# How much of the room for sorted tokens is zeroed, and when, in two routed feed-forward layers

## The chip, the core and the metric

The kernel runs on one core of a Trainium2 chip. A core has five engines with an instruction stream each: TensorE (PE, matmuls), VectorE (DVE), ScalarE (ACT), GpSimd (POOL) and SyncE (SP, which here only issues DMAs and loads registers). They meet by semaphores. DMAs run on 16 DMA engines that all issuers share. The metric is the device time of one execution in microseconds, the median of several.

## The reference

Six residual sublayers on x of 32 batches x 128 tokens x 128 channels: an attention, a cross attention, a feed-forward layer with 8 experts, then the same three once more with 16 experts. The change touches the two routed layers only. What they compute:

```python
# layer 0 (8 experts, 2 of them for each token)
t = rms_norm(x) * norm_weight                      # 4096 tokens of 128
gate_scores, expert_idx = top_k(t @ gate_w.T, 2)
weights = softmax(gate_scores)
x = x + sum over the 2 experts e: weights * (gelu(t @ W1[e].T + B1[e]) @ W2[e].T + B2[e])

# layer 1 (16 experts, 1 of them for each token)
hidden = _layernorm(x)
top_val, e = top_k(hidden @ router_w.T, 1)
g, u = split(sigmoid(top_val) * hidden @ gate_up[e])
x = x + silu(hidden @ shared_gate.T) * (hidden @ shared_up.T) @ shared_down.T + u * silu(g) @ down[e]
```

## The kernel before

One program in six stages, one for each sublayer; stage 3 is the layer with 8 experts, stage 6 the one with 16. Batches are worked on in 8 groups of 4 (G = 4). The order of the work is written out by hand in the source: each engine has its own list of pieces for each step, and a stage's opening pieces are mixed into the stage before.

**How tokens are sorted.** In DRAM lies `sorted_tokens`, a room with a region of rows for each expert (in stage 3 of 2560 rows, in stage 6 of 4096), 65536 rows of 512 bytes in all. VectorE works out for each token the row it goes to (expert times region plus the count of earlier tokens of that expert), and GpSimd scatters the tokens there, 128 with each indirect DMA (L1979 in stage 3, L3400 in stage 6). When the counts of all tokens are known, VectorE's `settle` rounds each expert's count up to whole tiles of 128 rows and makes a list of tiles: 48 of them in each of the two stages, so that a last few are spare. SyncE then loads tile numbers into a register, two at a time (L1930, L3550), and fetches the tiles into SBUF (L1932, L3552). TensorE takes them in quads of four: it flips them (L2523, L3797), multiplies them with their experts' weights, and SyncE stores the result of each quad (L1945, L3562). At the end GpSimd gathers each token's result rows (L2044, L3583), and they are added to x.

**Why zeros.** Rows of a tile behind an expert's last token hold no token. They are multiplied with the rest and nobody reads the result, but they have to hold numbers. So the whole room is zeroed from a tile of zeros (`s_zero`, L1920): its lower part ahead of stage 3 (4 transfers, ahead of GpSimd's first scatter, which waits for the semaphore `cleared`), the rest (4 transfers) behind it, and the lower part once more when stage 3 has used it (4 transfers). GpSimd's first scatter in stage 6, and the start of stage 5, wait for `regions_cleared`.

**Stage 3 in its order.** Five of the groups are sorted (their scatters lie in the last half of stage 2), three are computed densely, with every expert. TensorE does eight dense units, then the 12 quads of sorted tiles, then 16 more dense units, in which GpSimd gathers the results of the sorted groups and stage 4 is opened. A dense group begins with the flip of its tokens (L2445), then come units of hidden layer (L2505) and output (L2515), the logits (L2452), and the flip of the weights (L2460).

**Stage 6 in its order.** TensorE does 12 chunks of the shared expert, in the middle of which the last tokens are routed and `settle` runs on VectorE (its first signal is L3671); then the 12 quads, then 20 more shared chunks (L3772, L3774, L3783), during which GpSimd gathers. SyncE waits for `first_rows_ready` and for the last scatter, loads six quads ahead, and then stores a quad and loads another one in turn.

Of the kernel before, what the change touches and what calls it, by code (L numbers as in the profile page):

```python
# [1670 lines left out]
CLEARINGS = 8  # L1671
# [17 lines left out]
CLEARINGS3 = 4  # L1689
CLEARINGS_AT = {2: (0, 1), 3: (2, 3), 4: (4,), 5: (5,), 6: (6,), 7: (7,)}  # L1690
# [44 lines left out]
def stage3(nc, core, w, a, sorted_dram, done_dram, regions_cleared, before, stack):  # L1735
# [48 lines left out]
    pairs = pairs_index = place = done = None  # L1784
# [41 lines left out]
    ALL_ROWS = E6 * REGION // P  # L1826
# [88 lines left out]
    LOWER = slice(0, E3 * REGION3)  # L1915

    def clear_rows(sp, region, k, done):
        count = (region.stop - region.start) // CLEARINGS3
        piece = sorted_dram[region.start + k * count:region.start + (k + 1) * count, :]
        sp.dma_start(piece.rearrange("(p j) d -> p (j d)", p=P).rearrange("p (r c) -> p r c", c=GT),  # L1920
                     zero[:, :].unsqueeze(1).to_broadcast([P, count * D // P // GT, GT])).then_inc(done, 16)

    def by_sync(sp):
# [4 lines left out]
        def load(q):  # L1928
            for n in range(q * G, (q + 1) * G, 2):
                pair = nc.sync.value_load(pairs_index[0:1, n // 2:n // 2 + 1], min_val=0, max_val=ALL_ROWS ** 2 - 1)  # L1930
                for k, tile in enumerate((pair & (ALL_ROWS - 1), pair >> ALL_ROWS.bit_length() - 1)):
                    sp.dma_start(rows[:, (n + k) % (FLIGHTS * G), :],  # L1932
                                 tiles_dram[bass.ds(tile & (ALL_ROWS - 1), 1), :, :].rearrange("k p d -> p (k d)")
                                 ).then_inc(rows_landed[q % FLIGHTS], 16)

        sp.wait_ge(pairs_ready, 1)
        sp.wait_ge(dispatched, SORTED * G * 2 * 16)
# [282 lines left out]
    def by_vector(dve, piece, following=None):  # L2220
# [64 lines left out]
        def rank_of(g):  # L2285
# [13 lines left out]
            link(nc.vector.scalar_tensor_tensor(slot[:, :, :], index[:, batches, :], float(REGION3), rank[:, tens, :],  # L2299
# [3 lines left out]
        def settle():  # L2303
# [3 lines left out]
            def link(instruction):  # L2307
# [5 lines left out]
            dve.wait_ge(drained, turn["counts", 0] + 1)  # L2313
            link(nc.vector.tensor_scalar(padded[:, 0, :], counts[:, :], float(P - 1), None, ALU.add))
# [3 lines left out]
            link(nc.vector.tensor_scalar(gaps[:, :], padded[0:1, 1, :], -1.0, float(REGION3), ALU.mult, ALU.add))  # L2318
            tile_start = w.tile_start[:, :].unsqueeze(2).to_broadcast([1, TILES3, E3 - 1])
            link(nc.vector.tensor_tensor(passed[:, :, :],  # L2320
                                         ends[0:1, 0:E3 - 1].unsqueeze(1).to_broadcast([1, TILES3, E3 - 1]), tile_start,
                                         ALU.is_le))
            link(nc.vector.tensor_tensor(skipped[:, :, :], passed[:, :, :],
                                         gaps[:, 0:E3 - 1].unsqueeze(1).to_broadcast([1, TILES3, E3 - 1]), ALU.mult))
            link(nc.vector.tensor_reduce(owner[:, 1, :], skipped[:, :, :], AX.X, ALU.add))
            link(nc.vector.tensor_tensor(owner[:, 1, :], owner[:, 1, :], w.tile_start[:, :], ALU.add))
            link(nc.vector.tensor_scalar(owner[:, 1, :], owner[:, 1, :], float(E3 * REGION3 - P), None, ALU.min))
# [4 lines left out]
            link(nc.vector.tensor_reduce(owner[:, 0, :], passed[:, :, :], AX.X, ALU.add))  # L2332
# [296 lines left out]
    def main(following):  # L2629
        nonlocal b1_all, b2_all, h, padded, ends, starts, gaps, passed, skipped, owner, owners, owners_index, pairs, pairs_index  # L2630
        nonlocal place, done
        with ExitStack() as local:
# [8 lines left out]
            starts = late("starts", [P, E3])  # L2641
# [1320 lines left out]
```

## Time and profile before

| | |
|---|---|
| median of three runs | 1554.5 us (1547.81 to 1556.99) |
| the profiled execution's own time | 1555.21 us |
| its span, first to last instruction | 1553.4 us |
| mean granted TensorE clock | 0.965 |
| TensorE busy (matmuls) | 1429.2 us, 92% |
| VectorE, ScalarE, GpSimd busy | 59%, 53%, 43% |
| the chain that ended last | TensorE 58%, issue 14%, GpSimd 11% |
| DMA | 92.61 MB, 58.21 MB of them written to DRAM |

How to read it: the profile is of one execution, and its times are microseconds from the span's start. A row's idle time in brackets is what its engine waited just before, with what ended the wait; "issue" and "remote" say that nothing which the profile shows on this core's engines ended it. The clock column gives the granted TensorE clock as a share of 2.4 GHz (0.50 is 1.2 GHz). A row that stands for several instructions gives their count (x4). "us to landing" is the time from a DMA's issue to its completion.

### The profile page before, as it was taken

To read this page: it belongs to the slowest core of one execution; us is meant where nothing else is said; L and a number is where in the kernel's file an instruction comes from. 1 tells how busy PE (TensorE), PEld (TensorE's weight loads), DVE (VectorE), ACT (ScalarE), POOL (GpSimd) and SP (SyncE) were. 2 spreads that over 40 slices of the span, in tenths; PEclk is the share of its full clock that TensorE was granted. 3 is DMA by queue.
4 is the path that set the end of the run, shared out by engine and by line. 5 is a ranking of instruction groups with operands and counts; after the bars stand their busy time and mean duration, and the time that the engine had idled before them with its cause. 6 is when DMAs were issued, how large, how long until landed. Compare 5 with 4: busy or idle time off the path is not lost.

```text
span 1553.4 us, 38336 instructions
## 1 busy us (share of the span) xinstructions
PE 1429.2 (92%) x14613; PEld 1090.7 (70%) x14613; DVE 923.2 (59%) x2386; ACT 819.9 (53%) x1558; POOL 661.6 (43%) x679
## 2 busy tenths in 40 slices
PE   6999999996999988997968998989999999998997
PEld 5776776774777766795646666667778778775764
DVE  3343444334888864542488999965667667665223
ACT  4455455444686754453437776655554554542531
POOL 3234444434235543003478776623333444443034
PEclk9999999998999988998979999999999999999999
DMA  5020330000375631138100000000000000001323
GB/s 157 16 62 9 97 111 8 12 1 6 141 280 183 235 115 56 50 99 310 32 11 6 2 2 2 2 14 6 2 6 9 11 11 9 7 12 37 101 69 87
DMA packets 97821, 92.61 MB, mean 60 GB/s; under 512 B 21869, under 2 KB 71658, under 8 KB 97386
## 3 DMA queue, kind: packets, MB, share of 16 engines
q1 hardware_dynamic: 93034, 80.71, 16.0%
q0 software_dynamic: 4608, 9.45, 2.0%
q8 instruction: 120, 1.97, 0.5%
q14 instruction: 59, 0.48, 0.1%
HBM read 31.92 MB, written 58.21 MB: 58 GB/s over the span
## 4 chain that ended last, share of the span: by engine, by line
PE 58%; issue 14%; POOL 11%; DVE 7%; ACT 5%; DMA 3%; SPq 1%; another core or an unknown queue 1%; POOLq 0%; DVEq 0%; ACTq 0%
PE bank L3122 6%; PE bank L1538 5%; PE bank L3110 5%; PE bank L3157 4%; PE bank L1554 4%; PE bank L3136 4%; POOL s_p L1217 3%; PE bank L3148 3%; PE bank L854 2%; PE bank L2505 2%; PE bank L874 2%; PE bank L2515 2%; PE bank L827 2%; PE bank L1527 2%; POOL s_rows L3583 2%
## 5 line engine op out<-in xcount | busy, mean ns | idle before, releaser
L1324 ACT COPY s_pT<-bank 77x512 f32<-77x512 f32 (+1 forms) x256 | 136.4, 584 | 89.6 <-PE bank L1538 85.9
L2899 POOL TENSOR_TENSOR s_p<-s_p,s_inverse 128x616 f32<-128x616 f32 x64 | 78.6, 1230 | 216.0 <-DVE s_inverse L3037 216.0
L1538 PE MATMUL bank<-ident,s_p 128*77 128x128 f32 (+1 forms) x1024 | 147.5, 293 | 19.8 <-ACT s_p L1315 10.3
L1538 PEld LDWEIGHTS bank<-ident,s_p 128*77 128x77 f32 (+1 forms) x1024 | 122.0, 154 | 51.0 <-ACT s_p L1315 29.1
L1217 POOL TENSOR_TENSOR s_p<-s_p,s_peak 128x1024 f32<-128x1024 f32 x64 | 120.2, 1900 | 31.1 <-DVE s_peak L1408 31.1
L1315 ACT ACTIVATE s_p<-s_p 128x616 f32<-128x616 f32 (+1 forms) x128 | 111.0, 887 | 30.3 <-POOL s_p L1217 25.9
L720 DVE TENSOR_TENSOR s_aT<-bank,s_weight 128x512 f32<-128x512 f32 x64 | 44.3, 692 | 98.7 <-PE bank L864 82.3
L3122 PE MATMUL bank<-pos_bias,s_ctx 128*32 128x128 f32 x3072 | 91.9, 274 | 1.2 <-issue 1.2
L2957 ACT ACTIVATE s_p<-s_p 128x616 f32<-128x616 f32 x64 | 46.5, 726 | 85.7 <-DVE s_p L3025 85.7
L1394 DVE TENSOR_TENSOR s_p<-bank,pos_bias 128x1024 f32<-128x1024 f32 x64 | 77.7, 1218 | 20.9 <-PE bank L1527 20.9
L3021 DVE TENSOR_REDUCE s_peak<-bank 128x8 f32<-128x616 f32 x64 | 50.8, 794 | 62.8 <-PE bank L3136 62.8
L3122 PEld LDWEIGHTS bank<-pos_bias,s_ctx 128*32 128x32 f32 x3072 | 82.1, 110 | 6.5 <-issue 2.7
L3110 PE MATMUL bank<-s_ctx,s_kq 128*128 128x308 f32 x256 | 84.1, 437 | 1.8 <-ACT s_kT L2937 1.8
L1554 PE MATMUL bank<-s_pT,s_v 77*32 77x128 f32 (+1 forms) x2048 | 72.9, 283 | 12.9 <-DVE x_all L1441 12.0
L712 DVE TENSOR_TENSOR s_weight<-s_decay,bank 128x512 f32<-128x512 f32 x64 | 41.1, 683 | 73.4 <-ACT s_decay L560 73.4
L1527 PE MATMUL bank<-w_s_q,w_s_oT 32*128 32x308 f32 (+1 forms) x512 | 65.2, 580 | 19.0 <-POOL w_s_q L1208 15.3
L566 ACT COPY s_qT<-bank 128x512 f32<-128x512 f32 x64 | 37.5, 586 | 85.3 <-PE bank L827 85.3
L1554 PEld LDWEIGHTS bank<-s_pT,s_v 77*32 77x32 f32 (+1 forms) x2048 | 54.7, 112 | 36.8 <-issue 27.2
L3136 PE MATMUL bank<-s_kT,s_xnT 128*128 128x308 f32 x256 | 72.9, 426 | 6.3 <-ACT s_xnT L2930 6.3
L854 PEld LDWEIGHTS bank<-s_level,w_band 128*128 128x128 f32 x512 | 59.6, 191 | 26.3 <-issue 19.7
L3032 DVE TENSOR_REDUCE s_total<-s_p 128x8 f32<-128x616 f32 x64 | 50.1, 783 | 46.5 <-ACT s_p L2957 46.5
L2044 POOL DMA_INDIRECT s_tokens<-routed_tokens,s_done_index x40 | 38.4, 959 | 90.0 <-DMA routed_tokens<-s_routed 66.1
(364 smaller groups left out, 3526.2 us busy)
## 6 DMA issues: line engine op xcount, KB each, us to landing
sorted_tokens<-s_zero SPq DMA_DIRECT2D x4, 5632.0 KB
sorted_tokens<-s_zero SPq DMA_DIRECT2D x8, 2560.0 KB, 13.3
routed_tokens<-s_routed SPq DMA_DIRECT2D x24, 256.0 KB, 2.3
s_tokens<-sorted_tokens SPq DMA_DIRECT2D x48, 64.0 KB, 1.8
s_rows<-sorted_tokens SPq DMA_DIRECT2D x48, 64.0 KB, 1.9
x_all<-x SPq DMA_DIRECT2D x8, 256.0 KB, 3.3
w_s_gateup<-s_gateup SPq DMA_DIRECT2D x1, 2048.0 KB
out<-x_all SPq DMA_DIRECT2D x8, 256.0 KB
```

What stands on the lines that cost most here:

```text
L854: last = nc.tensor.matmul(bank[:, LEVEL + j, c * H1 * TB:(c + 1) * H1 * TB], w.band[:, start:start + T], level[:, b % 2, a, :, :].rearrang ...
L1217: nc.gpsimd.tensor_tensor(part, part, peak[:, b % 2, HU * u:HU * (u + 1)].unsqueeze(2).to_broadcast([P, HU, keys]), ALU.subtract).then_inc ...
L1315: nc.scalar.activation(part, part, ACT.Exp).then_inc(exp_ready, 1)
L1324: nc.scalar.copy(pT[0:keys, b % 2, 4 * q:4 * q + 4, :].rearrange("m h t -> m (h t)"), bank[0:keys, flip_bank("p", b, q), :]).then_inc(drai ...
L1394: nc.vector.tensor_tensor(p[:, b % 2, HU * u:HU * (u + 1), :].rearrange("p h m -> p (h m)"), scores_at(u).rearrange("p g c -> p (g c)"), b ...
L1527: last = nc.tensor.matmul(bank[:, SCORE + r, 0:LANES * keys], qT[rows, b % G * T:(b % G + 1) * T], own[rows, b % 2, :, :].rearrange("p j m ...
L1538: last = nc.tensor.transpose(bank[0:keys, into, j * T:(j + 1) * T], p[:, b % 2, 4 * q + j, :], core.ident[:, :])
L1554: last = nc.tensor.matmul(bank[LANE * r:LANE * (r + 1), WORK, at_column:at_column + T], of_lane(r, j), pT[0:keys, b % 2, LANES * r + j, :] ...
L2899: nc.gpsimd.tensor_tensor(part, part, inverse[:, b % 2, heads].unsqueeze(2).to_broadcast([P, HU, M]), ALU.mult).then_inc(share_ready, 1)
L3110: nc.tensor.matmul(bank[:, into, 0:GM].rearrange("p (n m) -> p n m", m=M), kq[:, h, :], ctx[:, g % 3, :, LEFT:LEFT + M], start=True, stop= ...
L3122: last = nc.tensor.matmul(bank[lane:lane + LANE, into[q], tile % QUAD * D:(tile % QUAD + 1) * D], ctx[:, g % 3, b % G, column:column + LAN ...
L3136: last = nc.tensor.matmul(bank[:, SCORE5 + q, 0:QUAD * M].rearrange("p (h m) -> p h m", m=M), xnT[:, n * T:(n + 1) * T], kT[:, g % 2, QUAD ...
```

## The change

The room gets a stride of region plus 128 rows for each expert, so that 128 rows behind any last token lie in the expert's own region; it grows to 1024 tiles. The twelve transfers of L1920 go. In their place:

- In stage 2, with the last group's context, SyncE zeroes only the spare tiles of both stages (8 and 16 tiles, two transfers).
- `settle` works out, before anything else, the first row behind each expert's last token (`pad_rows`; two VectorE steps).
- As soon as these are there, SyncE loads them into a register one by one, 8 in stage 3 and 16 in stage 6, and zeroes 128 rows from each on. Its tile loads wait, besides for what they waited for, until these have landed.
- GpSimd's first scatters no longer wait for a clearing. The tile list compares with one expert more (so that spare tiles are found behind the last region).

```diff
-CLEARINGS = 8
+STRIDE = REGION + P
+ROW_BASE = 1024
+SPACE = ROW_BASE * P
...
-    def clear_regions(sp, g):
...
-        for k in CLEARINGS_AT[g]:
-            if k < CLEARINGS3:
-                clear_rows(sp, LOWER, k, cleared)
-            else:
-                clear_rows(sp, slice(E3 * REGION3, E6 * REGION), k - CLEARINGS3, regions_cleared)
...
+    def clear_spare_tiles(sp, g):
+        if g != GROUPS - 1:
+            return
         sp.wait_ge(zero_ready, 1)
+        for spare, tiles, done in ((E3 * STRIDE3, E3, cleared), (E6 * STRIDE, E6, regions_cleared)):
+            sp.dma_start(
+                sorted_dram[spare:spare + tiles * P, :].rearrange("(p j) d -> p (j d)", p=P).rearrange(
+                    "p (r c) -> p r c", c=GT),
+                zero[:, :].unsqueeze(1).to_broadcast([P, tiles * D // GT, GT])).then_inc(done, 16)
...
+        sp.wait_ge(settled, PADS_SETTLED)
+        for e in range(E3):
+            row = nc.sync.value_load(pad_rows[0:1, e:e + 1], min_val=0, max_val=e * STRIDE3 + REGION3)
+            sp.dma_start(sorted_dram[bass.ds(row, P), :], zero[:, 0:D]).then_inc(cleared, 16)
         sp.wait_ge(pairs_ready, 1)
+        sp.wait_ge(cleared, (1 + E3) * 16)
         sp.wait_ge(dispatched, SORTED * G * 2 * 16)
...
-        for k in range(CLEARINGS3):
-            clear_rows(sp, LOWER, k, regions_cleared)
...
-                if g == DENSE:
-                    pool.wait_ge(cleared, CLEARINGS3 * 16)
...
+            link(nc.vector.scalar_tensor_tensor(pad_starts[:, :], w.s3_count[0:1, :], float(STRIDE3), counts[0:1, :],
+                                                ALU.mult, ALU.add))
+            link(nc.vector.tensor_copy(pad_rows[:, :], pad_starts[:, :]))
             link(nc.vector.tensor_scalar(padded[:, 0, :], counts[:, :], float(P - 1), None, ALU.add))
...
+        self.nc.gpsimd.memset(self.zero[:, :], 0.0)
...
-                if g == 0:
-                    pool.wait_ge(self.regions_cleared, CLEARINGS * 16)
...
+            sp.wait_ge(settled, 1)
+            for e in range(E6):
+                row = nc.sync.value_load(pad_rows[0:1, e:e + 1], min_val=0, max_val=e * STRIDE + REGION)
+                sp.dma_start(sorted_dram[bass.ds(row, P), :], route.zero[:, :]).then_inc(regions_cleared, 16)
             sp.wait_ge(first_rows_ready, 1)
+            sp.wait_ge(regions_cleared, (1 + E6) * 16)
             for k in range(2):
                 sp.wait_ge(route.dispatched[k], GROUPS // 2 * G * 16)
...
+                nc.vector.scalar_tensor_tensor(pad_starts[:, :], w.s6_count[0:1, :], float(STRIDE),
+                                               bank[0:1, ring.bank("total", 0), 0:E6], ALU.mult, ALU.add)
                 nc.vector.tensor_scalar(padded[:, 0, :], bank[:, ring.bank("total", 0), 0:E6], float(P - 1), None,
                                         ALU.add).then_inc(ring.drained, 1)
                 dve.wait_ge(ring.drained, ring.place["total", 0] + 1)
+                nc.vector.tensor_copy(pad_rows[:, :], pad_starts[:, :])
                 nc.vector.tensor_scalar(padded[:, 1, :], padded[:, 0, :], 7, 7, ALU.logical_shift_right,
                                         ALU.logical_shift_left).then_inc(settled, 1)
...
-                engine.wait_ge(regions_cleared, CLEARINGS * 16)
+                engine.wait_ge(regions_cleared, 16)
```

SyncE's order at the end of stage 3, before: the last stores of quads, the clearing, and the next stage's context.

```order
L1945 DMA routed_tokens<-s_routed 128x4x128 [waits s3_out_used] x5
L1920 DMA sorted_tokens<-s_zero 1280x1x512 x4
L1632 UNCONDITIONAL_BRANCH
L2866 DMA s_ctx<-ctxT 128x4x77 [waits semaphores_set_back,regions_cleared,s2_x_ready]
L2866 DMA s_ctx<-ctxT 128x4x77 x2
```

And in the changed kernel, whose lines are numbered anew:

```order
L1927 ISA
L1927 DMA s_tokens<-sorted_tokens 128x128
L1945 DMA routed_tokens<-s_routed 128x4x128 [waits s3_out_used] x5
L1632 UNCONDITIONAL_BRANCH
L2867 DMA s_ctx<-ctxT 128x4x77 [waits semaphores_set_back,regions_cleared,s2_x_ready]
L2867 DMA s_ctx<-ctxT 128x4x77 x2
```

```order
L3545 UNCONDITIONAL_BRANCH
L3550 TENSOR_LOAD s_pairs_index [waits s1_lam_landed,s1_operands_ready,s6_first_rows_ready,s5_x_ready]
L3550 ISA x2
L3552 REGISTER_ALU x2
L3552 ISA
L3552 DMA s_rows<-sorted_tokens 128x128
L3552 REGISTER_ALU x2
L3552 ISA
L3552 DMA s_rows<-sorted_tokens 128x128
L3550 TENSOR_LOAD s_pairs_index
```

In the changed kernel it begins with the pads; the first of the sixteen and the last, with what follows:

```order
L3546 UNCONDITIONAL_BRANCH
L3558 TENSOR_LOAD s_pad_rows [waits s6_settled,s5_x_ready]
L3558 ISA x2
L3559 ISA
L3559 DMA sorted_tokens<-s_zero 128x128
```

```order
L3558 TENSOR_LOAD s_pad_rows
L3558 ISA x2
L3559 ISA
L3559 DMA sorted_tokens<-s_zero 128x128
L3551 TENSOR_LOAD s_pairs_index [waits s1_lam_landed,s1_operands_ready,regions_cleared,s6_first_rows_ready]
L3551 ISA x2
L3553 REGISTER_ALU x2
L3553 ISA
L3553 DMA s_rows<-sorted_tokens 128x128
```

Sixteen register loads and sixteen DMAs now stand ahead of the first load of a tile, which has one semaphore more to wait for (the names beginning with s1_ are semaphores used again, here for the scatters). Stage 3 has eight such pads at the same place, ahead of its first tile load.

## Rows read from the trace of the kernel before

**Rows 1.** DMA issues of the page: out<-in, engine, count, KB each, us to landing.

```profile
sorted_tokens<-s_zero SPq DMA_DIRECT2D x4, 5632.0 KB
sorted_tokens<-s_zero SPq DMA_DIRECT2D x8, 2560.0 KB, 13.3
```

**Rows 2.** Stretches: length, engines' busy us (instructions), clock, DMA share, GB/s.

```profile
405.00:420.00 15.00, 14.91 (x267) 11.68 (x267) 12.63 (x28) 11.49 (x23) 2.63 (x3) 1.00 0.98 359
516.00:524.00 8.00, 7.21 (x77) 5.74 (x78) 6.03 (x18) 4.07 (x9) 4.82 (x6) 0.58 1.04 369
708.00:738.00 30.00, 23.22 (x115) 16.30 (x114) 7.47 (x39) 10.72 (x21) 15.19 (x16) 0.83 1.04 385
1491.00:1541.00 50.00, 49.59 (x234) 30.89 (x232) 18.02 (x28) 11.12 (x19) 28.29 (x30) 1.00 0.23 59
```

**Rows 3.** Timeline of TensorE: start, length, line, tiles, count, [idle before].

```profile
620.52 1.06 PE L2445 MATMUL bank<-ident,s_tokens 128*128 128x128 f32 x4
...
633.96 0.60 PE L2460 MATMUL bank<-ident,s_combine 128*8 128x128 f32 x4
...
715.75 1.02 PE L2445 MATMUL bank<-ident,s_tokens 128*128 128x128 f32 x4
...
738.71 0.60 PE L2460 MATMUL bank<-ident,s_combine 128*8 128x128 f32 x4
```

**Rows 4.** Timeline of ScalarE and TensorE between the last two of these.

```profile
722.53 0.69 ACT L2091 ACTIVATE s_dense_xnT<-bank,w_s_norm 128x512 f32<-128x512 f32 x1 [4.47 <-remote]
...
728.88 1.22 PE L2515 MATMUL bank<-w_s_w2T,s_hT 128*128 128x128 f32 x4 [2.16 <-issue]
```

**Rows 5.** Timeline of TensorE, behind 1541 us.

```profile
1542.01 3.84 PE L3783 MATMUL bank<-w_s_sdownT,s_shared 128*128 128x128 f32 x32 [1.41 <-issue]
```

**Rows 6.** DMA queues of the page: packets, MB, share of 16 engines.

```profile
q8 instruction: 120, 1.97, 0.5%
```

**Rows 7.** Timeline of VectorE in stage 2.

```profile
516.35 0.29 DVE L1441 TENSOR_TENSOR x_all<-bank,x_all 128x128 f32<-128x128 f32 x1 [2.27 <-issue]
...
577.02 0.96 DVE L1429 RECIPROCAL s_inverse<-bank 128x128 f32<-128x128 f32 x1 [7.71 <-remote]
```

**Rows 8.** Chain of waits, 1472 to 1479 us: start, length, piece.

```profile
1473.12 0.26 SPq L3550
...
1474.63 0.34 SPq L3552
...
1475.00 0.27 SPq L3550
...
1475.85 0.33 SPq L3552
...
1476.52 1.93 DMA s_rows<-sorted_tokens
```

**Rows 9.** Timeline of VectorE, stage 6: the step with the first signal.

```profile
1419.74 0.17 DVE L3671 TENSOR_SCALAR s_padded<-s_padded 128x16 int32<-128x16 int32 x1
```

**Rows 10.** SyncE's line 3550: ns min/median/max, first and last start.

```profile
L3550 SPq TENSOR_LOAD <-s_pairs_index x24: 264/272/283, 1426.0 to 1475.0; - x24
```

**Rows 11.** Timeline of SyncE, stage 6.

```profile
1450.09 0.39 SPq L3562 DMA_DIRECT2D routed_tokens<-s_routed  x1
...
1476.90 0.97 SPq L3562 DMA_DIRECT2D routed_tokens<-s_routed  x2
```

**Rows 12.** Timeline of TensorE: the flip of the last four rows.

```profile
1478.58 0.63 PE L3797 MATMUL bank<-ident,s_rows 128*128 128x128 f32 x4 [0.61 <-DMA s_rows<-sorted_tokens]
```

**Rows 13.** Timeline of GpSimd: its first gather of stage 6.

```profile
1491.99 1.00 POOL L3583 DMA_INDIRECT s_rows<-routed_tokens,s_done_index  x1 [67.33 <-DMA routed_tokens<-s_routed]
```

**Rows 14.** Timeline of VectorE, stage 3: the second step of settle.

```profile
622.00 0.17 DVE L2315 TENSOR_SCALAR s_padded<-s_padded 128x8 int32<-128x8 int32 x1
```

**Rows 15.** SyncE's line 1930, columns as in rows 10.

```profile
L1930 SPq TENSOR_LOAD <-s_pairs_index x24: 262/270/488, 625.1 to 685.9; - x24
```

**Rows 16.** Timeline of TensorE: the flips of the first two quads.

```profile
640.96 1.04 PE L2523 MATMUL bank<-ident,s_tokens 128*128 128x128 f32 x8
```

More of the change, by code:

```diff
@@ L1688 @@
 REGION3 = SORTED * GT
-CLEARINGS3 = 4
-CLEARINGS_AT = {2: (0, 1), 3: (2, 3), 4: (4,), 5: (5,), 6: (6,), 7: (7,)}
+STRIDE3 = REGION3 + P
+PADS_SETTLED = 2
 FLIGHTS = 4
@@ L1783, in stage3 @@
     b1_all = b2_all = h = padded = ends = starts = gaps = passed = skipped = owner = owners = owners_index = None
-    pairs = pairs_index = place = done = None
+    pairs = pairs_index = place = done = pad_starts = pad_rows = None
     def sem(name):
@@ L2630, in main @@
         nonlocal b1_all, b2_all, h, padded, ends, starts, gaps, passed, skipped, owner, owners, owners_index, pairs, pairs_index
-        nonlocal place, done
+        nonlocal place, done, pad_starts, pad_rows
         with ExitStack() as local:
@@ L2641, in main @@
             starts = late("starts", [P, E3])
+            pad_starts = late("pad_starts", [1, E3])
+            pad_rows = late("pad_rows", [1, E3], I32)
             gaps = late("gaps", [1, E3])
-            passed = late("passed", [1, TILES3, E3 - 1])
-            skipped = late("skipped", [1, TILES3, E3 - 1])
+            passed = late("passed", [1, TILES3, E3])
+            skipped = late("skipped", [1, TILES3, E3])
             owner = late("owner", [1, 2, TILES3])
@@ L2684, in stage3 @@
                   work_bank=lambda pe: pe.wait_ge(out_used, LAST), gather=gather)
-    return Opening(clear_regions, by_gpsimd, by_scalar, by_vector, by_tensor, main), after
+    return Opening(clear_spare_tiles, by_gpsimd, by_scalar, by_vector, by_tensor, main), after
 FILTERS, TAPS, RES = 4, 101, 64
@@ L3248, in __init__ @@
         self.no_rows = sbuf("no_rows", [P, E6])
+        self.zero = sbuf("zero", [P, D])
         self.earlier = sbuf("earlier", [P, P], BF16)
@@ L3459, in by_tensor, with stage6 @@
                                  stop=True).then_inc(ring.filled, 1)
-def stage6(nc, core, w, route, out, sorted_dram, done_dram, x_from):
+def stage6(nc, core, w, route, out, sorted_dram, done_dram, regions_cleared, x_from):
     with ExitStack() as local:
@@ L3476, in stage6 @@
         starts = sbuf("s6_starts", [P, E6])
+        pad_starts = sbuf("s6_pad_starts", [1, E6])
+        pad_rows = sbuf("s6_pad_rows", [1, E6], I32)
         gap = sbuf("s6_gap", [1, E6])
@@ L3506, in stage6 @@
         LOADED = 6
-        ALL_ROWS = E6 * REGION // P
         tiles_dram = sorted_dram.rearrange("(k p) d -> k p d", p=P)
@@ L3549, in load @@
                 for n in range(q * G, (q + 1) * G, 2):
-                    pair = nc.sync.value_load(pairs_index[0:1, n // 2:n // 2 + 1], min_val=0, max_val=ALL_ROWS ** 2 - 1)
-                    for k, tile in enumerate((pair & (ALL_ROWS - 1), pair >> ALL_ROWS.bit_length() - 1)):
-                        sp.dma_start(rows[:, n + k, :], tiles_dram[bass.ds(tile & (ALL_ROWS - 1), 1), :, :].rearrange(
+                    pair = nc.sync.value_load(pairs_index[0:1, n // 2:n // 2 + 1], min_val=0, max_val=ROW_BASE ** 2 - 1)
+                    for k, tile in enumerate((pair & (ROW_BASE - 1), pair >> ROW_BASE.bit_length() - 1)):
+                        sp.dma_start(rows[:, n + k, :], tiles_dram[bass.ds(tile & (ROW_BASE - 1), 1), :, :].rearrange(
                             "k p d -> p (k d)")).then_inc(rows_landed[q], 16)
+            sp.wait_ge(settled, 1)
+            for e in range(E6):
+                row = nc.sync.value_load(pad_rows[0:1, e:e + 1], min_val=0, max_val=e * STRIDE + REGION)
+                sp.dma_start(sorted_dram[bass.ds(row, P), :], route.zero[:, :]).then_inc(regions_cleared, 16)
             sp.wait_ge(first_rows_ready, 1)
+            sp.wait_ge(regions_cleared, (1 + E6) * 16)
             for k in range(2):
@@ L3684, in settle @@
                 nc.vector.tensor_tensor(skipped[:, :, :], passed[:, :, :],
-                                        gap[:, 0:E6 - 1].unsqueeze(1).to_broadcast([1, TILES6, E6 - 1]),
+                                        gap[:, :].unsqueeze(1).to_broadcast([1, TILES6, E6]),
                                         ALU.mult).then_inc(settled, 1)
@@ L3886, in laid_out @@
     out["owner_digit"] = (float(E6) ** (np.arange(TILES6) % G)).astype(np.float32)
-    out["row_digit"] = (float(E6 * REGION // P) ** (np.arange(TILES6) % 2) / P).astype(np.float32)
+    out["row_digit"] = (float(ROW_BASE) ** (np.arange(TILES6) % 2) / P).astype(np.float32)
     for k, name in enumerate(("q", "k", "v")):
@@ L3904, in program @@
     bias_dram = nc.dram_tensor("bias_scratch", [H, SPAN], F32, kind="Internal").ap()
-    sorted_dram = nc.dram_tensor("sorted_tokens", [E6 * REGION, D], F32, kind="Internal").ap()
+    sorted_dram = nc.dram_tensor("sorted_tokens", [SPACE, D], F32, kind="Internal").ap()
     done_dram = nc.dram_tensor("routed_tokens", [TILES6 * P, D], F32, kind="Internal").ap()
```

50 lines of the change are left out of this document (21 added, 29 removed).

## The prediction

> **What bounds the kernel now.** I read the page first: the chain that ended last runs mostly through TensorE, so a DMA or a VectorE step counts only where TensorE is kept waiting for it. The list of DMA issues shows what the change is about: twelve transfers of the zero tile, four of 5632 KB and eight of 2560 KB, 43 MB of writes [rows 1]. In the timeline of SyncE they stand at two places: four of 2560 KB and four of 5632 KB in stage 2 (405 to 420 and 516 to 524 us are two such stretches), and four of 2560 KB at the end of stage 3 (708 to 738 us). The busy time by stretches shows what they do there: the 16 DMA engines are full (share 0.98 to 1.04, about 360 to 385 GB/s), against 0.23 in a stretch without them [rows 2].
>
> Full DMA engines are not yet lost time. In 405 to 420 us they are full, and TensorE is busy 14.91 of 15.00 us at the full clock level, 2.4 GHz [rows 2]. So the question is where a wait in such a stretch ends late; I looked for waits that end on "issue" or "remote", that is, on nothing that another engine did.
>
> **What is removed, end of stage 3.** The same program piece runs twice in stage 3: flip the tokens of a dense group (L2445), two units, the logits, two or three units more, flip the combine weights (L2460). The first time it takes from 620.52 to 633.96, 13.4 us; the second time, under the clearing, from 715.75 to 738.71, 23.0 us [rows 3]. The 9.5 us between them are gaps: ScalarE idle for 4.47 us though its bank was filled, and TensorE idle for 2.16 us ahead of single matmuls [rows 4]. In this stretch GpSimd also gathers rows by indirect DMA, so the clearing isn't the only suspect. The stretch that has gathers and no clearing is 1491 to 1541 us: TensorE is busy 49.59 of 50.00 us [rows 2], and the one gap right behind it is 1.41 us [rows 5]. So I put gathers alone at 1.4 us and the clearing at 9.5 - 1.4 = 8.1 us gained (bounds: 0, if the gaps are the gathers'; 9.5, if all of it goes). TensorE is what everything up to stage 4 waits for here, so I count it in full.
>
> On the blocks of instructions, which come over the same DMA engines: the page has a queue of its own for them, 120 packets and 1.97 MB, some 16 KB each [rows 6]. I take the gaps of [rows 4] for such blocks that come late behind the zeros; that is a guess, since no row names what the engines waited for. The Trainium skill ("DMA: Bandwidth & Descriptors", section "Queues, rings and completion order") speaks against it: each DMA engine takes turns between the queues, a packet at a time, so a block would wait for one packet of the clearing and not for its backlog. By that rule the gaps would stay and the gain would be about nothing; 405 to 420 us agrees with it, 715 to 739 us does not.
>
> **What is removed, stage 2.** Here the clearing runs beside the scatters of the sorted rows. VectorE stands idle for 2.27 us on "issue" in such a stretch (three such gaps, 2.05 to 2.28 us, 6.6 us in all), but the longest of the kind, 7.71 us, ends at 577 us, behind the last clearing of this stage, beside scatters alone [rows 7]. By that nearest row the scatters make these gaps, and I take 0. Upper bound: all three gaps go, and with each the stretch at the lower clock level that follows it (8 us at a granted clock of 0.58, at most 8 x 0.42 = 3.4 us [rows 2]): 6.6 + 3 x 3.4 = 17 us. Lower bound 0: a transfer that isn't made slows nothing here.
>
> **What is added, stage 6.** SyncE gets 16 steps ahead of its row loads: load a start from SBUF into a register, issue 64 KB of zeros. The price is in the loads that it already issues: register load at 1473.12, its second row DMA at 1474.63, the next register load at 1475.00, that one's first DMA at 1475.85 [rows 8]. So 0.85 us from register load to DMA and 0.37 us from there to the next register load, 1.22 us. A pad has two register steps fewer; between the two DMAs stand four and 0.34 us beside the DMA's own 0.33, so some 0.08 each: 1.06 us a pad. Sixteen take 15 x 1.06 + 0.7 = 16.6 us to the last issue, and a 64 KB transfer lands 1.93 us behind its issue [rows 8] (a read; for the write I take the same): 18.5 us.
>
> They start when VectorE has the counts: the shift that ends in the first signal starts at 1419.74 and takes 0.17 [rows 9]; the two added VectorE steps put it at about 1420.2. So the first row load can follow at 1438.7, where it now stands at 1426.0 [rows 10], where the last scatter lands: 12.7 us later. Bounds for it: 0.95 us a pad gives 11, 1.22 gives 15.
>
> Does that reach the end? From 1450.09 to 1476.90 SyncE issues a store and four loads for each of six quads, 4.47 us each, of which one has a slow issue [rows 11]; TensorE waits for the last loads (0.61 us [rows 12]). So SyncE already sets the pace there and can't catch up, but for the slow issue: about 0.9 us. Behind the loads: the last store, on which GpSimd's gathers wait 67.33 us [rows 13], and behind these the sums and the output. All of it moves. I take 12 us (10 to 15). In these 12 us nothing else is late: the scatters have landed, and VectorE has long signalled `first_rows_ready`.
>
> **What is added, stage 3.** Eight pads in the same way: 7 x 1.06 + 0.7 + 1.93 = 10 us from the second signal of `settle`, which now comes at 622.2 [rows 14] and stays there (two steps of 0.2 us take the place of two): the row loads start at 632.3 in place of 625.1 [rows 15]. The loads of the first two quads then land at about 637.6 and 641.4; TensorE flips them from 640.96 on, the second one 0.4 us later [rows 16]. So its cover is just long enough. I take 0.5 us with the longer `settle` (bounds 0 and 3: each 0.1 us more a pad makes the second flip wait 0.7 us). With that cover gone it would cost up to 7 us.
>
> **At nothing:** the added memset on GpSimd and the spare tiles' 1.5 MB, both far ahead of their use; the waits that GpSimd loses ahead of its first scatters, which ended long before; one more column in the VectorE comparisons (SyncE is still at its pads).
>
> **Sum.** The profiled execution took 1555.2 us (span 1553.4 and 1.8 around it): + 12 + 0.5 - 8.1 = 1559.6. The median of the runs lies 0.7 us below the profiled one: 1559 us, 0.3% above before. Own range of this case: 1554 to 1564.
>
> **Rivals.**
> 1. Slower. The gaps at 715 to 739 us are the gathers', or the fetches' own, and stay; SyncE's 16 pads remain as a pure loss: 1554.5 + 12.5 = 1567 us. For it: the 7.71 us gap beside scatters alone [rows 7], and the full DMA engines that harm nothing at 405 us [rows 2]. Against it: gathers alone in stage 6 leave TensorE nearly without a gap [rows 2]. It decides from where less than 4.7 us of the 9.5 go (12.5 less the 7.8 us that are 0.5%). The arbitration rule of the Trainium skill named above leads here too. Chance 0.25.
> 2. Faster. The clearing is also behind the gaps of stage 2, with the clock that falls behind each: 1559 - 17 = 1542 us if all goes, 1550 if half does. For it: the three gaps come only in stretches where clearing and scatters meet, and the clock is at the full level under the clearing alone. Against it: 577 us. It decides from three quarters of the 17 us on. Chance 0.15.
> 3. That the row loads of stage 6 aren't held up to the end: if TensorE and not SyncE sets the pace behind 1450 us, it makes up the half of the delay: 1553 us. Rows 12 speak against it. I count it into the forecast's range.
>
> **How the numbers follow.** Forecast 0.60, rival 1 0.25, rival 2 0.15. What this measurement can tell from no change is about 0.5%, 7.8 us: below 1546.7 faster, above 1562.3 slower. Of the forecast 0.10 lies above 1562.3 (pads of 1.2 us, or a gap that stays in part) and the rest within; of rival 1 0.22 above; of rival 2 0.13 below (some of the forecast's edge adds 0.01). Faster 0.14, same 0.54, slower 0.32. Range: 1546 to 1568, which leaves out the far half of rival 2 and the cases of rival 1 with slow pads.
>
> **What would show it.** Right: in the profile after, the stretch from the flip of the tokens to the flip of the combine weights (715 to 739 us before) takes 14 to 15 us; the first row load of stage 6 is 12 to 13 us behind the last scatter's landing, and TensorE waits for rows from the first quad on; the gaps beside scatters in stage 2 are still there. Wrong: the second dense group keeps its 23 us (rival 1); the steps beside scatters in stage 2 shrink by more than 1 us each, with the clock at its full level there (rival 2); pads cheaper than 0.9 us or a TensorE that has caught up with the row loads by the last quad (stage 6 mis-sized).

## The result, and the profile after

The changed kernel takes 1570.6 us in the median of four runs (1569.49 to 1575.19), the kernel before 1555.18 us beside it (1547.81 to 1556.99): a ratio over all runs of 1.0123 with a 95% interval of 1.0095 to 1.0152 (the two medians alone give 1.0099). It is slower by 1.0 to 1.2%, where 1559 us and no change that can be measured was forecast. The profiled executions took 1569.49 us (span 1567.7) and 1555.21 us (span 1553.4), so 14.3 us are to be found in the traces.

That the change does what it says is seen in the DMA lines of the page; they answer to [rows 1].

```profile
DMA packets 80382, 51.72 MB, mean 33 GB/s; under 512 B 22093, under 2 KB 74954, under 8 KB 79946
...
sorted_tokens<-s_zero SPq DMA_DIRECT2D x24, 64.0 KB, 1.6
```

92.61 MB became 51.72; the twelve large transfers are gone, 24 pads of 64 KB are there, and a pad lands 1.6 us behind its issue. The stretches of [rows 2] at the same times (length, busy us and instructions of TensorE, its weight loads, VectorE, ScalarE and GpSimd, granted clock, DMA share, GB/s):

```profile
405.00:420.00 15.00, 14.91 (x262) 11.75 (x264) 11.59 (x27) 12.49 (x24) 2.62 (x3) 1.00 0.05 13
516.00:524.00 8.00, 6.31 (x84) 5.44 (x84) 6.43 (x21) 5.46 (x12) 4.19 (x6) 0.79 0.09 30
708.00:738.00 30.00, 23.93 (x113) 16.50 (x112) 6.78 (x35) 10.77 (x22) 15.15 (x16) 0.83 0.16 44
```

At 708 to 738 us the DMA share fell from 1.04 to 0.16, and TensorE is busy 23.93 us instead of 23.22, at the same mean clock of 0.83. The load that the forecast blamed is gone, and the stretch is as bad as it was. At 516 to 524 us the clock rose from 0.58 to 0.79, but that is not the missing clearing either. In the runs below, e3 without the clearing of stage 2 has 0.57 there, and e6 with it has 1.00 (the same columns, first e3, then e6):

```profile
516.00:524.00 8.00, 7.40 (x78) 5.88 (x79) 5.50 (x17) 3.91 (x9) 5.01 (x6) 0.57 0.07 26
516.00:524.00 8.00, 5.71 (x95) 4.44 (x96) 6.79 (x23) 7.54 (x16) 4.31 (x6) 1.00 1.03 369
```

TensorE's timeline of the two dense groups, against [rows 3]:

```profile
620.00 1.06 PE L2444 MATMUL bank<-ident,s_tokens 128*128 128x128 f32 x4
...
632.69 0.60 PE L2459 MATMUL bank<-ident,s_combine 128*8 128x128 f32 x4
...
716.72 1.02 PE L2444 MATMUL bank<-ident,s_tokens 128*128 128x128 f32 x4
...
739.79 0.60 PE L2459 MATMUL bank<-ident,s_combine 128*8 128x128 f32 x4
```

The second group takes 23.1 us (739.79 - 716.72), as before the change; the first takes 12.7, against 13.4. The longest gaps of the second have grown rather than gone: ScalarE's is 5.81 us, against 4.47 [rows 4], and TensorE's, ahead of the matmuls that read what ScalarE wrote there, 4.43 us, against 3.08. In all TensorE is idle for 6.1 us of this group, against 6.8. ScalarE's and TensorE's timeline, with the idle time before each row in brackets:

```profile
724.85 0.69 ACT L2087 ACTIVATE s_dense_xnT<-bank,w_s_norm 128x512 f32<-128x512 f32 x1 [5.81 <-remote]
725.69 1.85 PE L2451 MATMUL bank<-w_s_gateT,s_dense_xnT 128*128 128x8 f32 x8 [4.43 <-issue]
```

Nor did a block of instructions arrive late here. The queues of the DMA view for 718 to 726 us, whole (packets, MB, share):

```profile
q0 software_dynamic: 195, 0.41, 17.7%
```

Only GpSimd's gathers move; the instruction queues have no packet in the gap. In stage 2, the gaps of VectorE that [rows 7] shows are still there without the clearing (of the other two, one comes again with 2.44 us, and the one of 2.05 us as two of 1.05 and 1.15):

```profile
517.25 0.29 DVE L1441 TENSOR_TENSOR x_all<-bank,x_all 128x128 f32<-128x128 f32 x1 [2.44 <-issue]
...
577.59 0.96 DVE L1429 RECIPROCAL s_inverse<-bank 128x128 f32<-128x128 f32 x1 [7.82 <-remote]
```

What was added is where it was expected (the last row of each pair goes on; the window ends there). SyncE's timeline, pads and the row loads behind them, in stage 3 and stage 6:

```profile
622.66 8.48 SPq L1934 DMA_DIRECT2D sorted_tokens<-s_zero  x8
633.34 6.77 SPq L1927 DMA_DIRECT2D s_tokens<-sorted_tokens  x8
...
1421.99 17.79 SPq L3559 DMA_DIRECT2D sorted_tokens<-s_zero  x16
1441.88 4.15 SPq L3553 DMA_DIRECT2D s_rows<-sorted_tokens  x5
```

In stage 6 the first row load stood at 1426.9 us and stands at 1441.88. TensorE waits for the first rows and for the last (against [rows 12]):

```profile
1446.39 1.09 PE L3806 MATMUL bank<-ident,s_rows 128*128 128x128 f32 x4 [5.84 <-DMA s_rows<-sorted_tokens]
...
1493.49 0.63 PE L3806 MATMUL bank<-ident,s_rows 128*128 128x128 f32 x4 [1.30 <-DMA s_rows<-sorted_tokens]
```

The last flip came at 1478.58 and now comes at 1493.49, 14.9 us later. About 1.1 us of it was there when stage 6 began (the first step of `settle` begins at 1420.63 us, the first one before the change stood at 1419.54), 13.8 us arose in stage 6, and the end of the span moved by 14.3 us.

### The profile page after: what moved, and what is told of

The parts are those of the page before. It is cut to its first block, busy times and chain, and to the rows that moved or that the text cites. A ratio compares the mean times of both kernels' runs of the same rounds, so it can differ in the third digit from the quotient of the medians.

```text
span 1567.7 us, 38478 instructions
## 1 busy us (share of the span) xinstructions
PE 1428.6 (91%) x14613; PEld 1089.0 (69%) x14613; DVE 922.7 (59%) x2390; ACT 819.9 (52%) x1558; POOL 660.8 (42%) x680
## 2 busy tenths in 40 slices
DMA packets 80382, 51.72 MB, mean 33 GB/s; under 512 B 22093, under 2 KB 74954, under 8 KB 79946
## 4 chain that ended last, share of the span: by engine, by line
PE 56%; issue 15%; POOL 10%; DVE 7%; ACT 4%; SPq 4%; DMA 2%; another core or an unknown queue 1%; DVEq 0%; POOLq 0%; ACTq 0%
PE bank L3123 5%; PE bank L3111 5%; PE bank L1538 4%; PE bank L3158 4%; PE bank L3137 4%; PE bank L1554 4%; POOL s_p L1217 4%; PE bank L3149 3%; PE bank L854 2%; PE bank L874 2%; PE bank L827 2%; PE bank L2504 2%; PE bank L1527 2%; PE bank L833 1%; PE bank L864 1%
## 5 line engine op out<-in xcount | busy, mean ns | idle before, releaser
L1554 PE MATMUL bank<-s_pT,s_v 77*32 77x128 f32 (+1 forms) x2048 | 71.9, 280 | 15.9 <-DVE x_all L1441 13.4
```

What stands on the lines that cost most here:

```text
L1554: last = nc.tensor.matmul(bank[LANE * r:LANE * (r + 1), WORK, at_column:at_column + T], of_lane(r, j), pT[0:keys, b % 2, LANES * r + j, :] ...
```

## Experiments

The open question was what makes the second dense group 23 us long: the clearing (the forecast), or the gathers that GpSimd issues back to back at the same time. Of the others two price the pads, and the rest follow the answer to a faster kernel. Times are medians; the kernel before, run beside them, had 1553.5 us (e1 to e4), 1553.7 (e5 to e8), 1553.4 (e9, e10) and 1551.0 (e11).

**e1, the clearing alone taken away.**

```diff
-CLEARINGS = 8
+CLEARINGS = 4
...
-        for k in range(CLEARINGS3):
-            clear_rows(sp, LOWER, k, regions_cleared)
```

> The kernel before without the four transfers that clear the lower part of the room at the end of stage 3 (stage 6 then finds the numbers that stage 3 left there); no pads. The theory of the prediction (the clearing makes the gaps in the second dense group): the stretch from the flip of the tokens to the flip of the weights falls from 23.0 us to about 15, the time by 8 us to about 1547. Rival (the gaps have another cause, the gathers first of all): the stretch keeps 22 to 24 us, and the time is that of before within 2 us, about 1555.

1554.3 us, ratio 1.0011 (0.9993 to 1.0029): no change. TensorE's timeline:

```profile
712.84 1.02 PE L2443 MATMUL bank<-ident,s_tokens 128*128 128x128 f32 x4
...
736.32 0.60 PE L2458 MATMUL bank<-ident,s_combine 128*8 128x128 f32 x4
```

23.5 us. The clearing at the end of stage 3 cost nothing, and the forecast's 8.1 us were never to be had.

**e2, the changed kernel without the pads of stage 6.** The whole room is zeroed once in stage 2.

```diff
...
+        count = E6 * (STRIDE + P) // 8
+        for k in {2: (0, 1), 3: (2, 3), 4: (4,), 5: (5,), 6: (6,), 7: (7,)}.get(g, ()):
...
-            for e in range(E6):
-                row = nc.sync.value_load(pad_rows[0:1, e:e + 1], min_val=0, max_val=e * STRIDE + REGION)
-                sp.dma_start(sorted_dram[bass.ds(row, P), :], route.zero[:, :]).then_inc(regions_cleared, 16)
```

> The changed kernel without the 16 pads ahead of SyncE's row loads in stage 6; the whole room is zeroed once in stage 2 instead, in eight transfers, and the eight pads of stage 3 stay. If the pads in SyncE's queue make the whole loss of stage 6: the first row load stands right behind the last scatter again, and the time is 13 to 14 us below the changed kernel, about 1557. Rival (the larger stride, the longer list of tiles and the other steps of settle cost something too): it stays 5 us or more above that, 1562 or slower. Should the clearing in stage 2 cost time beside the scatters, it is seen in the steps of stage 2 here and not in the changed kernel.

1553.9 us, ratio 1.0012 (0.9996 to 1.0029). The 16 pads are the loss, within what can be measured: stride, longer list, the pads of stage 3 and 35 MB of zeros beside the scatters of stage 2 together leave nothing above about 0.3%.

**e3, plain transfers in place of the gathers of stage 3.**

```diff
-            nc.gpsimd.indirect_dma_start(
-                out=rows[:, j % 2 * 2 * G + 2 * n + k, :], out_offset=None, in_=done_dram[:, :],
-                in_offset=bass.IndirectOffsetOnAxis(ap=done_index[:, b, k:k + 1], axis=0)).then_inc(gathered[j % 2], 16)
+            pool.dma_start(rows[:, j % 2 * 2 * G + 2 * n + k, :],
+                           done_dram[(2 * b + k) * P:(2 * b + k + 1) * P, :]).then_inc(gathered[j % 2], 16)
```

> The changed kernel, in which stage 3 fetches fixed rows of its results with plain transfers from GpSimd's queue, of the same size and number and at the same places, instead of gathering each token's rows by index: the sums of the sorted groups get the wrong rows. If the index gathers make the gaps: the second dense group (23.1 us in the changed kernel) falls to 13 to 15 us, and the time by 8 to 10 us, to about 1561. Rival (the gaps come from something else in this stretch, or from any transfer then): it keeps 22 us or more, and the time stays at 1570.

1556.6 us, ratio 1.0018 (0.9999 to 1.0036), 14 us below the changed kernel and 4 us lower than expected; the second group gives 10.5 of the 14. GpSimd's timeline, and TensorE's:

```profile
711.54 8.68 POOL L2040 DMA_DIRECT2D s_tokens<-routed_tokens  x16 [69.67 <-DMA routed_tokens<-s_routed]
```

```profile
717.95 1.02 PE L2443 MATMUL bank<-ident,s_tokens 128*128 128x128 f32 x4
...
730.51 0.60 PE L2458 MATMUL bank<-ident,s_combine 128*8 128x128 f32 x4
```

Sixteen transfers in half the time, and the group takes 12.6 us. In 710 to 735 us the DMA view counts the same for both kernels on GpSimd's queue, 512 packets and 1.05 MB; so it isn't the bytes that hold the engines up, nor the number of transfers, it is the transfers by index. A plain transfer is also shorter on GpSimd, 8.68 us for sixteen where the gathers take some 20; this run doesn't tell the index from the time that it takes.

**e4, the gathers paced by TensorE.**

```diff
         for k in range(FIRST, UNITS3):
...
+            pool.wait_ge(expert_done, at(k))
             bring_back(pool, DENSE + (k - FIRST) // G, (k - FIRST) % G)
```

> The changed kernel, in which GpSimd waits ahead of each pair of gathers of stage 3 until TensorE has ended the unit before, so that 16 gathers no longer run back to back but two with each unit of about 4 us. If the burst of gathers makes the gaps of the second dense group: they shrink, the group takes 14 to 17 us instead of 23.1 and the time falls by 6 to 9 us. If each gather costs its own part wherever it lies: the same time within 2 us, the gaps spread over the units. If the gaps are not the gathers': the group keeps 23 us, or the added wait makes it longer.

1561.7 us, ratio 1.0071 (1.0050 to 1.0093), 9 us below the changed kernel. GpSimd's timeline shows a pair for each unit, and TensorE's the group:

```profile
726.70 0.94 POOL L2041 DMA_INDIRECT s_tokens<-routed_tokens,s_done_index  x1 [1.96 <-PE bank L2515]
727.95 0.95 POOL L2041 DMA_INDIRECT s_tokens<-routed_tokens,s_done_index  x1 [0.31 <-issue]
730.21 0.94 POOL L2041 DMA_INDIRECT s_tokens<-routed_tokens,s_done_index  x1 [1.31 <-PE bank L2515]
```

```profile
717.50 1.02 PE L2445 MATMUL bank<-ident,s_tokens 128*128 128x128 f32 x4
...
730.13 0.60 PE L2460 MATMUL bank<-ident,s_combine 128*8 128x128 f32 x4 [0.20 <-DVE s_combine L2274]
```

12.6 us with all gathers still made. So a gather has no fixed price wherever it lies; the price goes with the burst.

**e5 and e6, the kernel before with paced gathers**, without the clearing (e5) and with it (e6). e6 has the last edit alone.

```diff
-CLEARINGS = 8
+CLEARINGS = 4
...
-        for k in range(CLEARINGS3):
-            clear_rows(sp, LOWER, k, regions_cleared)
...
+            pool.wait_ge(expert_done, at(k))
             bring_back(pool, DENSE + (k - FIRST) // G, (k - FIRST) % G)
```

> The kernel before without the clearing at the end of stage 3 and with the gathers of stage 3 paced by TensorE's units, as in the run of the changed kernel with paced gathers; no pads. If the burst of gathers alone makes the gaps: the second dense group takes 12 to 14 us instead of 23, and the time falls 8 to 10 us below the kernel before, to about 1545, faster than both kernels. If the gain of the paced gathers was bound to the changed kernel (its delayed stage 6): about 1554.

> The kernel before with its clearing at the end of stage 3 kept and the gathers paced. If full DMA engines harm nothing there: the second dense group takes 12 to 14 us under the clearing too, and the time is that of the run without this clearing, about 1545. If the clearing and the gathers together are to blame (zeros that delay the gathers' transfers): the group stays at 16 us or more, and the time at 1548 or above.

e5: 1540.4 us, ratio 0.9927 (0.9904 to 0.9949). e6: 1540.9 us, ratio 0.9922 (0.9902 to 0.9942). Both gain 13 us, 3 to 5 more than expected, and the clearing makes no difference. The group itself gives 10.4 us (12.6 in place of 23.0). In the trace of e6 it ends 11.1 us earlier than in the kernel before (727.60 us against 738.71), `settle` of stage 6 begins 12.1 us earlier and the span is 13.9 us shorter; what makes the last 3 us is not known. The stretch of e6 to set beside [rows 2] (same columns as above):

```profile
708.00:738.00 30.00, 29.82 (x170) 21.22 (x170) 13.53 (x62) 14.86 (x28) 16.11 (x17) 1.00 1.03 379
```

The DMA engines are as full as before (1.03, 379 GB/s), and TensorE is busy 29.82 of 30 us at a clock of 1.00, where it had 23.22 at 0.83.

**e7, twice the pads in stage 6.**

```diff
+            for e in range(E6):
+                row = nc.sync.value_load(pad_rows[0:1, e:e + 1], min_val=0, max_val=e * STRIDE + REGION)
+                sp.dma_start(sorted_dram[bass.ds(row + P, P), :], route.zero[:, :]).then_inc(regions_cleared, 16)
...
-            sp.wait_ge(regions_cleared, (1 + E6) * 16)
+            sp.wait_ge(regions_cleared, (1 + 2 * E6) * 16)
```

> The changed kernel with 16 more register loads and pads ahead of the row loads of stage 6 (each 128 rows further on). If the pads' issue on SyncE is the price: sixteen more cost 16 x 1.16 = 18.6 us in the first row load and the same at the end, about 1588. If the price is the landing of the zeros, or SyncE makes the delay good behind it: less than 10 us more, 1580 or below.

1588.3 us, ratio 1.0225 (1.0198 to 1.0252), 17.7 us above the changed kernel. SyncE's timeline:

```profile
1424.28 18.84 SPq L3559 DMA_DIRECT2D sorted_tokens<-s_zero  x16
1443.89 17.16 SPq L3562 DMA_DIRECT2D sorted_tokens<-s_zero  x16
1463.16 6.71 SPq L3553 DMA_DIRECT2D s_rows<-sorted_tokens  x8
```

Each pad is a step of 1.1 to 1.2 us in SyncE's queue, and hardly any of it is made good: the first row load is 21.3 us later than in the changed kernel, and the last flip, at 1513.95 us, 20.5 us (1.9 us of both were there when stage 6 began).

**e8, the scatters at the head of stage 3 paced too** (on top of e5).

```diff
                 if step + n // 2 >= BATCH:
+                    pool.wait_ge(expert_done, min(n + 1, 4))
                     dispatch(g, n)
```

> As the kernel before without the clearing at the end of stage 3 and with paced gathers, and the burst of eight scatters at the head of stage 3 (603 to 613 us) paced too, two with each of the first units. If bursts of indexed transfers hold up ScalarE in general: its gap of 7 us at 615 us goes, and the first group's weights are flipped 2 to 4 us earlier, about 1542. If that gap has another cause: no change against the run with paced gathers alone, or slower where the rows land later.

1535.6 us, ratio 0.9900 (0.9878 to 0.9923), 4.8 us below e5. The first group's weights are flipped 5.2 us earlier than there (624.41 us against 629.59), somewhat more than the 2 to 4 us expected. ScalarE's step behind the burst of eight scatters, in the kernel before and in e8:

```profile
614.96 0.59 ACT L2120 COPY s_total<-bank 128x512 f32<-128x512 f32 x1 [7.04 <-remote]
```

```profile
606.57 0.58 ACT L2120 COPY s_total<-bank 128x512 f32<-128x512 f32 x1 [2.28 <-PE bank L2489]
```

The gap of 7 us is gone; what is left ends with TensorE's result, as it should.

**e9, the scatters of stage 2 spread as well** (on top of e8): one batch, two scatters, for each step instead of two batches in each of two steps; what is left over is paced at the head of stage 3.

```diff
-SENT_AT = {step + k: (g, (2 * k, 2 * k + 1)) for step, g in sent_at(18).items() for k in range(2) if step + k < BATCH}
+SENT_AT = {step + k: (g, (k,)) for step, g in sent_at(18).items() for k in range(G) if step + k < BATCH}
...
+        units = iter((0, 1, 1, 2, 3, 4))
...
-                if step + n // 2 >= BATCH:
-                    pool.wait_ge(expert_done, min(n + 1, 4))
+                if step + n >= BATCH:
+                    unit = next(units)
+                    if unit:
+                        pool.wait_ge(expert_done, unit)
                     dispatch(g, n)
```

> As the run in which the gathers and the scatters at the head of stage 3 are paced, and the scatters of stage 2 spread too: two in each step of that stage instead of four in each of two steps (the rest go to the head of stage 3, where TensorE's units pace them). If bursts of indexed transfers are behind the gaps of stage 2 as well: VectorE's gap of 7.6 us at 577 us and the 2.3 us gaps before it go, and the time falls by 5 to 15 us below 1535.6. If those gaps are a step's own (its waits on TensorE and ScalarE): the same time, 1534 to 1538, or slower where the rows of the first quads land later.

1530.4 us, ratio 0.9847 (0.9818 to 0.9876): the fastest, and faster than both kernels. It is 5.2 us below e8, at the edge of what was expected. In the kernel before, eight scatters stand back to back from 565 to 575 us, and TensorE's timeline reads so:

```profile
568.20 0.43 PE L1554 MATMUL bank<-s_pT,s_ones 77*32 77x128 f32 x5 [0.29 <-issue]
568.93 0.41 PE L1554 MATMUL bank<-s_pT,s_ones 77*32 77x128 f32 x4 [0.31 <-issue]
569.68 0.41 PE L1554 MATMUL bank<-s_pT,s_ones 77*32 77x128 f32 x4 [0.34 <-issue]
```

Four or five matmuls, a halt of 0.3 us that nothing in the profile ends, and again, until VectorE has stood idle for 7.71 us [rows 7]. In e9 that step of VectorE:

```profile
569.71 0.96 DVE L1429 RECIPROCAL s_inverse<-bank 128x128 f32<-128x128 f32 x1 [1.86 <-PE bank L1554]
```

The long gap is gone, though four scatters still stand in a row there and TensorE halts three times (0.31 to 1.01 us). Of the shorter gaps one of 2.51 us is left, at 515.61 us, but it is of another kind: VectorE's step starts 0.1 us behind the end of the TensorE step (L1564) that it reads, where in the kernel before that step had ended 2.9 us earlier (at 513.47, and VectorE began at 516.35). Where the 5.2 us come from the traces don't show: the profiled execution of e9 took 1536.01 us, its slowest, and that of e8 1534.71.

**e10, the gathers spaced by GpSimd's own work** (the changed kernel with five memsets behind each pair).

```diff
...
             bring_back(pool, DENSE + (k - FIRST) // G, (k - FIRST) % G)
+            for i in range(5):
+                nc.gpsimd.memset(zero[:, :], 0.0).then_inc(spaced, 1)
+                pool.wait_ge(spaced, 5 * (k - FIRST) + i + 1)
```

> The changed kernel with each pair of gathers of stage 3 followed by five memsets of 0.5 us on GpSimd (a tile that is no longer used), and no wait for TensorE. It tells the space between the gathers from the place that the paced run gave them beside TensorE's units. If the space alone does it: the second dense group takes 12 to 15 us, and the time is that of the changed kernel with paced gathers, 1560 to 1563. If the wait for TensorE is what helps: the group keeps 20 us or more, about 1570.

1586.3 us, ratio 1.0212 (1.0178 to 1.0247): half right. The group takes 12.8 us, so space alone is enough for the group:

```profile
716.86 1.02 PE L2448 MATMUL bank<-ident,s_tokens 128*128 128x128 f32 x4
...
729.61 0.60 PE L2463 MATMUL bank<-ident,s_combine 128*8 128x128 f32 x4 [0.32 <-issue]
```

The time went up because GpSimd, kept busy by the memsets, opened stage 4 late: ScalarE waited 22.8 us for GpSimd there, and TensorE 18.9 us for ScalarE (in the changed kernel TensorE's longest wait in 735 to 900 us is 6.3 us).

```profile
767.22 1.65 ACT L1272 ACTIVATE w_s_v<-x_all,s_shift,s_rstd 128x128 f32<-128x128 f32 x4 [22.78 <-POOL s_shift L1202]
767.85 1.54 PE L1493 MATMUL bank<-ident,w_s_v 128*128 128x128 f32 x4 [18.85 <-ACT w_s_v L1272]
```

**e11, a wait for landing after every four gathers**, as stage 6 has it, on the changed kernel.

```diff
+        if n == 2:
+            pool.wait_ge(gathered[j % 2], (j // 2) * G * 2 * 16 + 2 * n * 16)
+        if n == 0 and j:
+            pool.wait_ge(gathered[(j - 1) % 2], ((j - 1) // 2 + 1) * G * 2 * 16)
```

> The changed kernel, in which GpSimd waits in stage 3, after every four gathers, until these have landed (as it does in stage 6, where TensorE has hardly a gap), and for nothing else. If it is the gathers under way at one time that hold the engines up: the second dense group takes 12 to 15 us and the time falls to 1560 to 1563. If only pairs spread over TensorE's units help (the share of time in which GpSimd gathers): the group takes 17 us or more, since fours with a wait of about 2 us between them still fill most of the time.

1562.7 us, ratio 1.0067 (1.0043 to 1.0091), as e4. GpSimd's timeline at the wait, and TensorE's:

```profile
720.11 0.94 POOL L2044 DMA_INDIRECT s_tokens<-routed_tokens,s_done_index  x1 [0.30 <-issue]
722.92 0.94 POOL L2044 DMA_INDIRECT s_tokens<-routed_tokens,s_done_index  x1 [1.87 <-DMA s_tokens<-routed_tokens,s_done_index]
```

```profile
715.98 1.02 PE L2448 MATMUL bank<-ident,s_tokens 128*128 128x128 f32 x4
...
728.77 0.60 PE L2463 MATMUL bank<-ident,s_combine 128*8 128x128 f32 x4 [0.36 <-DVE s_combine L2277]
```

12.8 us. Waits of 1.9 us after every four are enough, without any link to TensorE's units; that speaks for the number of gathers issued without a stop, not for the place that the gathers have beside TensorE's work.

## Why the prediction was wrong

1. **Removed, end of stage 3: -8.1 us forecast, nothing measured.** This is the step that failed. It gave the 9.5 us of gaps to the clearing, less 1.4 us for "gathers alone". The 1.4 us were read in stage 6 [rows 2, 5], but the two stretches don't hold the same thing: stage 3 issues sixteen gathers without a stop, stage 6 waits for landing after every four. GpSimd's timeline in the kernel before, one gather of stage 3, and one of stage 6 behind such a wait:

```profile
719.77 0.94 POOL L2044 DMA_INDIRECT s_tokens<-routed_tokens,s_done_index  x1 [0.30 <-issue]
...
1498.88 0.95 POOL L3583 DMA_INDIRECT s_rows<-routed_tokens,s_done_index  x1 [1.88 <-DMA s_rows<-routed_tokens,s_done_index]
```

e1 takes the clearing away and keeps the gaps; e3 puts plain transfers in the gathers' place, e4, e10 and e11 break up their burst, and all four lose the gaps; e6 keeps the clearing and loses them. The gaps were the burst's. Nor are the 9.5 us all gaps. The two groups before the change, in the columns of [rows 2]:

```profile
620.52:633.96 13.44, 13.31 (x74) 9.73 (x74) 10.79 (x55) 5.54 (x11) 0.00 (x0) 0.90 0.13 36
715.75:738.71 22.96, 16.18 (x74) 11.16 (x73) 5.71 (x34) 7.07 (x15) 10.40 (x11) 0.78 1.02 383
```

TensorE is idle for 6.8 us of the second and 0.1 of the first; the other 2.9 us are the same 74 matmuls, which took longer at a mean granted clock of 0.78 in place of 0.90. The guess that instruction blocks come late finds nothing: between 718 us and the end of the gaps none lands, before the change or after. The rule of the Trainium skill ("DMA: Bandwidth & Descriptors", section "Queues, rings and completion order"), that the DMA engines take turns between queues by the packet, would have left the gaps and the time where rival 1 had them; e6, with full DMA engines and 29.82 of 30 us of TensorE, agrees with it, though no run here shows the taking of turns itself.
2. **Removed, stage 2: 0, right.** The gaps stayed without the clearing, the clock at 516 to 524 us differs from kernel to kernel with it and without it (0.57 in e3, 1.00 in e6), and e2, with more of it, is no slower. Here the forecast read 577 us rightly as the scatters' work, and didn't carry that reading over to the gathers of stage 3. e9 shows that the long gap goes with the burst of eight.
3. **Added, stage 6: +12 us forecast, 13.8 measured; mechanism right, the size a little low.** The first pad's DMA to the last's took from 1422.0 to 1439.4 us, 1.16 us a pad and not 1.06 (the first five steps 1.29, for a reason that is not known, the other ten 1.10); the last zeros landed in 1.5 us and not 1.93; and the 0.9 us that SyncE was to catch up did not come, since the last flip is 14.9 us late. e7 doubled the pads and added 17.7 us.
4. **Added, stage 3: +0.5 us forecast, about 2 measured; mechanism right, size low.** The row loads begin at 633.34 us as worked out (632.3 and the register load). But TensorE came to the first flip 1.3 us earlier than before the change (639.69 us against 640.96), since its first group was shorter, and so waited 1.31 us for the second quad:

```profile
639.69 0.60 PE L2522 MATMUL bank<-ident,s_tokens 128*128 128x128 f32 x4
641.60 0.63 PE L2522 MATMUL bank<-ident,s_tokens 128*128 128x128 f32 x4 [1.31 <-DMA s_tokens<-sorted_tokens]
```

From the flip of the first group's weights to the flip of the second group's tokens it took 84.0 us, against 81.8 before (83.4 to 86.0 in the seven profiled kernels that have these pads, 81.4 to 82.9 in the six that have not). TensorE came to the second group 1.0 us later.

The sum of rival 1 (nothing gained at the end of stage 3, the pads as pure loss: 1567 us) is what happened, 2 to 4 us low through points 3 and 4, and the sign that the forecast had named for it, a second group that keeps its 23 us, is the one that came. Rival 2 (the clearing also behind the gaps of stage 2) and rival 3 (TensorE making up half of the delay in stage 6) are refuted by points 2 and 3.

## What to carry to other kernels

Before a gap is given to the transfer that fills the DMA engines, look for the same gap where that transfer is absent, and compare the other suspect in the same form (sixteen in a row against four and a wait), not only by name. Large transfers for which nothing waits can be free (43 MB here), while small ones that one queue has to issue ahead of what the next stage waits for are not: 24 transfers of 64 KB cost some 15 us. Break bursts of gathers and scatters by index with a wait, best one that the kernel needs anyway; this was worth 13 us in the gathers alone (e6) and 23 us in all (e9), more than anything in the change.

## What the hardware showed

Bursts of indexed transfers from GpSimd hold up the other engines: ScalarE for 5.81 us in a burst of 16 gathers and for 7.04 us in one of eight scatters, VectorE for 7.71 us in another of eight, and TensorE halts every four or five matmuls beside the latter. Beside groups of four scatters in stage 2 VectorE has gaps of 2.0 to 2.4 us; in e9, with pairs there, those that are left each end within 0.1 us of the TensorE step that VectorE reads. Groups of four gathers with a wait behind them leave the second group of stage 3 at 12.8 us (e11), and 16 plain transfers of the same bytes from the same queue at 12.6 us (e3). TensorE's clock follows: a mean of 0.83 in the stretch with the burst, 1.00 in e6. What the held engine waits for is not settled: the wait is put down to "issue" or "remote", no instruction block lands in it, and no run here looks inside GpSimd's issue.
